# Attention scores on Trainium2: the second pass of two query tiles on the two row halves of TensorE

## The reference, cut to what matters

```python
q = _apply_rope((xn @ Wq + bq).reshape(b, s, 16, 64), cos, sin)   # k alike, v without rope
scores = einsum('bnqd,bnkd->bnqk', q, k) / sqrt(64)
scores = where(causal, scores, -1e9)
attended = einsum('bnqk,bnkd->bnqd', softmax(scores), v)
x = x + attended @ Wo + bo + int8_ffn(xn)
```

## Time and profile before

| | |
|---|---|
| timed, median of 3 | 1139.77 us (1139.35 to 1143.02) |
| profiled execution | 1136.91 us |
| its span, first to last instruction | 1134.8 us |
| TensorE busy | 1029.4 us (91%) |
| VectorE busy | 875.1 us (77%) |
| GpSimd busy | 752.3 us (66%) |
| ScalarE busy | 697.0 us (61%) |
| scores' first pass, L1592 | 512 matmuls, 148.2 us busy |
| scores' second pass, L1593 | 512 matmuls, 154.1 us busy |
| mask, L1594 | 512 matmuls, 112.6 us busy |

### The profile page before, as it was taken

The page is one execution under the profiler, slowest core; times in us unless marked ns, Lnnn a source line. Parts: engine busy times, 40 slices in busy tenths (PEclk is TensorE's granted clock), DMA queues, the critical chain, the costliest instruction groups (busy, mean ns, idle before and its releaser), DMA issues.

```text
span 1134.8 us, 23158 instructions
## 1 busy us (share of the span) xinstructions
PE 1029.4 (91%) x7950; PEld 667.2 (59%) x7950; DVE 875.1 (77%) x1846; ACT 697.0 (61%) x1864; POOL 752.3 (66%) x936
## 2 busy tenths in 40 slices
PE   3559887989999999999999999999999775999998
PEld 1236555656667666676667666676667542444444
DVE  7877768867887777777777777777776638999996
ACT  2248885656666666666666666666667415667763
POOL 2456656758777877778677877778676335666762
PEclk9789998999999999999999999999999977999999
DMA  8533333433332233233333233322331000000001
GB/s 274 162 88 94 107 125 109 137 95 95 112 103 85 90 117 111 86 103 94 94 102 104 89 94 107 113 85 93 96 100 51 1 1 1 19 20 19 19 28 48
DMA packets 100276, 98.47 MB, mean 87 GB/s; under 512 B 13888, under 2 KB 96064, under 8 KB 99520
## 3 DMA queue, kind: packets, MB, share of 16 engines
q1 hardware_dynamic: 100160, 96.99, 27.3%
HBM read 56.05 MB, written 40.90 MB: 85 GB/s over the span
## 4 chain that ended last, share of the span: by engine, by line
PE 73%; DVE 17%; ACT 4%; issue 3%; DMA 1%; POOL 0%; SPq 0%; DVEq 0%; ACTq 0%; POOLq 0%
PE bank L1521 24%; PE bank L1605 13%; PE bank L1619 12%; PE bank L1636 8%; PE bank L1592 6%; PE bank L1593 6%; DVE arena L1407 3%; PE bank L1594 2%; PE bank L1786 2%; DVE nm L1377 1%; ACT arena L796 1%; DVE wmax L1060 1%; DVE arena L1426 1%; DVE nm L1231 1%; DVE arena L1391 1%
## 5 line engine op out<-in xcount | busy, mean ns | idle before, releaser
L610 POOL TENSOR_SCALAR arena<-arena,rc 128x128 f32<-128x128 f32 (+3 forms) x512 | 279.2, 563 | 206.4 <-DVE rc L1239 206.4
L796 ACT ACTIVATE arena<-bank,nm 128x256 f32<-128x256 f32 (+3 forms) x512 | 268.9, 528 | 93.5 <-DVE nm L1231 83.7
L1231 DVE TENSOR_REDUCE nm<-bank 128x1 f32<-128x256 f32 (+3 forms) x512 | 229.9, 481 | 94.2 <-PE bank L1594 90.8
L1605 PE MATMUL bank<-ident,arena 128*128 128x128 f32 x1280 | 217.5, 278 | 19.7 <-ACT arena L804 17.9
L1605 PEld LDWEIGHTS bank<-ident,arena 128*128 128x128 f32 x1280 | 145.4, 142 | 56.1 <-ACT arena L804 23.6
L804 ACT ACTIVATE arena<-bank 128x256 f32<-128x256 f32 (+3 forms) x272 | 118.8, 440 | 79.4 <-PE bank L1605 79.2
L1592 PE MATMUL bank<-arena 128*128 128x256 f16 (+3 forms) x512 | 148.2, 302 | 10.7 <-ACT arena L796 10.0
L1593 PE MATMUL bank<-arena 128*128 128x256 f16 (+3 forms) x512 | 154.1, 301 | 0.0
L1619 PE MATMUL bank<-arena 128*64 128x512 f32 (+3 forms) x1024 | 152.0, 439 | 0.0
L1246 DVE COPY arena<-bank 128x512 f32<-128x512 f32 (+1 forms) x240 | 115.6, 482 | 29.0 <-PE bank L1605 25.5
L1619 PEld LDWEIGHTS bank<-arena 128*64 128x64 f32 x1024 | 67.8, 136 | 94.3 <-issue 72.2
(11 more groups left out here) (157 smaller groups left out, 2202.5 us busy)
## 6 DMA issues: line engine op xcount, KB each, us to landing
arena<-scr SPq DMA_DIRECT2D x320, 128.0 KB, 2.6
scr<-arena SPq DMA_DIRECT2D x256, 128.0 KB, 1.7
arena<-in_weights SPq DMA_DIRECT2D x5, 1024.0 KB, 7.1
x_sb<-in_x SPq DMA_DIRECT2D x8, 512.0 KB, 9.7
out<-x_sb SPq DMA_DIRECT2D x16, 256.0 KB, 2.1
xscr<-arena SPq DMA_DIRECT2D x12, 256.0 KB, 3.0
xsh<-xscr SPq DMA_DIRECT2D x6, 256.0 KB, 3.3
xsl<-xscr SPq DMA_DIRECT2D x6, 256.0 KB, 4.7
```

The costliest lines, as they stand in the source:

```text
L610: last = pool.tensor_scalar(pr[slot][:, OFF[i]:OFF[i + 1]], pr[slot][:, OFF[i]:OFF[i + 1]], rc[:, slot, i:i + 1], 1.0, ALU.mult, ALU.mult)
L796: act.activation(pr[slot][:, OFF[i]:OFF[i + 1]], s_tile[i], ACT.Exp, bias=nm[:, slot, i:i + 1], accum_out=sm[:, slot, i:i + 1]).then_inc(e ...
L1231: dve.tensor_reduce(nm[:, slot, i:i + 1], s_tile[i], AX.X, ALU.max, negate=True).then_inc(max_done, 1)
L1605: last = pe.transpose(banks[5 + h][:, (i - j) * P:(i - j + 1) * P], pr[2 * par + h][:, OFF[i] + j * P:OFF[i] + (j + 1) * P], ident[:])
```

## The change

The zero rows of `kz` go: kl now lies in both halves. The second pass of a tile uses 64 rows alone, rows 0 to 63 for odd tiles and 64 to 127 for even ones, so that two tiles' passes lie on different rows of the array and in different banks. For that the query stacks of even tiles are swapped (ql above, qh below); the projection of queries puts even tiles first (`by_parity`, `token_tiles`), so that `move_queries` can place the halves, in eight fetches of half size instead of four; `move_keys` makes eight fetches instead of six. The rotation tables get the same order, and two memsets go from GpSimd. On every engine scores are handled in two groups per head, (1, 0) and (3, 2), instead of three. (1, 0) waits for exps 0, 1 and 2 of the previous head. (3, 2) waits for exp 0 of its own head (`4 * g + 1`), which shares the bank sy. Core of the diff:

```diff
-        S_BANK = {1: 1, 0: 2, 2: 2, 3: 3}
+        S_GROUP = {0: 1, 1: 1, 2: 2, 3: 2}
+        Q_AT = {0: 0, 2: 1, 1: 2, 3: 3}
...
+        def by_parity(a):
+            return a.rearrange("p (e t c) -> p e t c", e=2, t=2)
+        def token_tiles(a, odd):
+            return a if odd else a.rearrange("p (t e c) -> p e t c", t=2, e=2)
...
         move_queries:
-                    sp.dma_start(qs[par][piece * HL:(piece + 1) * HL],
-                                 scr[par, 0, piece].rearrange("(h r) s -> r h s", h=4)).then_inc(q_in[par], 16)
+                    rows = scr[par, 0, piece].rearrange("(h r) s -> r h s", h=4)
+                    for e in range(2):
+                        at = (piece * HL + L * (1 - e)) % P
+                        sp.dma_start(qs[par][at:at + HL, :, e * 2 * P:(e + 1) * 2 * P],
+                                     rows[:, :, e * 2 * P:(e + 1) * 2 * P]).then_inc(q_in[par], 16)
...
         move_keys:
-                    if piece < 2:
-                        sp.dma_start(kd[par][at:at + HL], rows).then_inc(k_in[par], 16)
-                        sp.dma_start(kd[par][L + at:L + at + HL], rows).then_inc(k_in[par], 16)
-                    else:
-                        sp.dma_start(kz[par][at:at + HL], rows).then_inc(k_in[par], 16)
+                    both = (kd, kd, kz, kz)[piece][par]
+                    sp.dma_start(both[at:at + HL], rows).then_inc(k_in[par], 16)
+                    sp.dma_start(both[L + at:L + at + HL], rows).then_inc(k_in[par], 16)
...
         GpSimd:
-            for par in range(2):
-                pool.memset(kz[par], 0.0).then_inc(kz_zero, 1)
...
         ScalarE, ring:
-                exps(n + 1, 0, e, (1,))
+                exps(n + 1, 0, e, (0, 1))
                 v_whole(n)
                 pt_whole(n, 0)
                 high_e(n + AHEAD - 1)
-                exps(n + 1, 0, e, (0, 2))
...
                 high_o(n + AHEAD - 1)
                 pt_whole(n, 1)
-                exps(n + 1, 0, e, (3,))
+                exps(n + 1, 0, e, (2, 3))
...
-                exps(n + 1, 1, e, (1, 0, 2))
+                exps(n + 1, 1, e, (0, 1))
                 pt_whole(n, 3)
-                exps(n + 1, 1, e, (3,))
+                exps(n + 1, 1, e, (2, 3))
...
         VectorE, ring:
-                maxima(n + 1, 0, e, (1,))
+                maxima(n + 1, 0, e, (0, 1))
                 out_low(n - 1)
-                maxima(n + 1, 0, e, (0, 2))
...
-                maxima(n + 1, 0, e, (3,))
+                maxima(n + 1, 0, e, (2, 3))
...
                 pt_whole(n, 1)
                 even_terms(n + AHEAD)
                 inverse(n + 1, 0, e)
-                maxima(n + 1, 1, e, (1,))
+                maxima(n + 1, 1, e, (0, 1))
...
                     pt_whole(n, 2)
-                maxima(n + 1, 1, e, (0, 2, 3))
+                maxima(n + 1, 1, e, (2, 3))
...
         TensorE, scores:
-                after(pe, exp_done, 4 * g - 4 + {1: 1, 0: 3, 3: 4}[tiles[0]])
+                after(pe, exp_done, 4 * g - 1 if tiles == (1, 0) else 4 * g + 1)
                 for i in tiles:
-                    out, q = s_tile[i], qs[par][:, hh, i * P:(i + 1) * P]
-                    pe.matmul(out, q, kd[par][:, hh, 0:(i + 1) * P], start=True, stop=False)
-                    pe.matmul(out, q, kz[par][:, hh, 0:(i + 1) * P], start=False, stop=False)
-                    last = pe.matmul(out[:, i * P:(i + 1) * P], identb[:], maskb[:], start=False, stop=True)
+                    q = qs[par][:, hh, Q_AT[i] * P:(Q_AT[i] + 1) * P]
+                    pe.matmul(s_tile[i], q, kd[par][:, hh, 0:(i + 1) * P], start=True, stop=False)
+                for i in tiles:
+                    half = slice(L * (1 - i % 2), L * (1 - i % 2) + L)
+                    pe.matmul(s_tile[i], qs[par][half, hh, Q_AT[i] * P:(Q_AT[i] + 1) * P], kz[par][half, hh, 0:(i + 1) * P],
+                              start=False, stop=False)
+                for i in tiles:
+                    last = pe.matmul(s_tile[i][:, i * P:(i + 1) * P], identb[:], maskb[:], start=False, stop=True)
                 last.then_inc(s_done, 1)
```

## The result

The changed kernel takes 1200.17 us, median of 4 runs (1198.37 to 1201.71), against 1139.71 for the kernel before on the same chip: a ratio of the means of 1.0523 (95% interval 1.0498 to 1.0548), slower. The forecast was 1195 us. The profiled execution took 1199.76 us, of which 1197.8 are its span, 63.0 more than before.

A forecast was written before the change was run, and what follows sets the result against it. TensorE was taken to bound the rings. Per ring -0.43 - 0.19 + 0.84 + 0.63 = +0.85, +43 over 51 rings; with +7, +2 and some 3 at the ends, +55: 1195 us, range 1180 to 1218.

The forecast's parts named there:

- What the pass saves: Scores on TensorE: side-by-side second passes save 512 columns, 0.21 us per head, 0.43 per ring.
- The rival that they run one after the other: Second passes in scores: halves in different banks don't run side by side; 1217 us, chance 0.10.
- Two changes of form per group: Scores on TensorE: 0.10 us per change, 0.21 per group with weight loading, 0.84 per ring.
- the changes are free: Scores on TensorE: changes to half of the rows cost nothing, the wait stays; 1151 us, chance 0.15.
- run under other matmuls: Scores on TensorE: half-row passes change form free and run under the full matmuls around them; 1117 us, chance 0.07.
- The wait: Head 1's (3, 2): TensorE stands 0.63 us per ring for exp 0 of its own head.
- E: The end of a ring's `evens` on TensorE, from which the forecast counts times in us.
- The wait given back at `pt` 1: Six transposes before `evens`: they no longer wait for VectorE's copy of `pt` 0 of head 1, 0.19 us less.
- Steady rings: Rings 8 to 58, with `evens`, scores and `attended`: +0.85 us per ring, +43 over 51 rings.
- Rings 59 to 62: Last rings with scores, without `evens`: (1, 0) of head 1 stands too, 4 x 1.8 = +7 us.
- Rings 0 to 7: First rings, where ScalarE copies for both heads: part of the wait given back, +0.3 us each, +2.
- Ring -1: Before ring 0: `evens` now stands behind exp 0, some 3 us later.

The follow-up runs named there:

- x2: Changed kernel with both second passes of a group on the same half, rows 0 to 63, so they can't run side by side: 1221.69 us, ratio 1.0734.
- x3: Kernel before, order and waits untouched, with each tile's second pass on rows 0 to 63 alone: 1226.09 us, ratio 1.0773.
- x4: Changed kernel with head 1's wait removed by order: exp 0 made earlier, (3, 2) ahead of `pt` 3; half rows stay: 1156.14 us, ratio 1.0161.
- x8: Kernel before with head 1's `pt` 1 transposes moved behind the first three of the six products of `evens`: 1118.69 us, ratio 0.9831.
- x6: Changed kernel with SyncE's store of x's columns ahead of the query fetches instead of behind them: 1193.21 us, ratio 1.0494.
- x5: Changed kernel with the second pass on all 128 rows and the order in which head 1's (3, 2) doesn't wait: 1136.64 us, ratio 1.0004.
- x7: Kernel before, with its own data, zero rows and DMAs, in the new order of two groups without head 1's wait: 1136.47 us, ratio 1.0003.
- x1: Changed kernel with its second pass on all 128 rows again; groups, waits and DMAs stay: 1178.32 us, ratio 1.0355.

## Why the prediction was right

The sign and the size came out of the sum, and its steps in the steady rings hold, one of them with some luck:

- **What the pass saves.** 0.43 per ring: x2 puts 0.16 per (3, 2) group back when the halves may not run side by side, and its ordinary rings grow by 0.44. The rival that they run one after the other falls.
- **Two changes of form per group.** 0.10 each on rows as on columns, though no stretch of the rings before had shown rows. It was right to price them by `av` and not by the setup's 0.17, which set the upper end of the range. The granted clock was 1.00 there too, so the clock is no reason against that row. But 0.17 is a distance of starts that holds the one-column matmul itself, and the two instructions of this matmul, of one form, already start 0.14 apart (46.71 and 46.85). Groups take 0.59 and 0.92, forecast were 0.60 and 0.92. By x3 and x4 the two rivals fall in which the changes are free, or run under other matmuls. The Trainium skill, "TensorEngine Tiling (Array Packing)", Key Properties, says that a change of mode drains TensorE; the gaps agree, on both axes.
- **The wait.** Forecast was (3, 2) at E + 2.43 and its end at E + 3.35; measured are 2.45 and 3.38. x4 shows that it binds: with exp 0 made earlier and (3, 2) ahead of `pt` 3, 0.65 per ring go. It was found by walking VectorE's queue from E on, and in an ordinary ring that is the chain that comes second. Exp 0 goes behind ScalarE's copy of `pt` 2, which the forecast had ahead of exp 0 in every fourth ring only. That copy hangs on TensorE, so x2's 0.05 was not hidden. The size is right to 0.02 because both chains end within 0.1 us of each other; that is luck.
- **The wait given back at `pt` 1.** Six transposes in 0.66, and x8 gets the same gain by itself.
- **Steady rings.** +0.85 forecast, +0.88 measured, and the same in every fourth ring, as said. Rings 9 to 58 took 45.1 more; 43 were forecast for these and ring 8.
- **Rings 59 to 62.** +7 forecast, +7.6 measured.

Three terms were mis-sized, all of them outside the steady rings:

- **Rings 0 to 7, +2.** Measured +7.3 for rings 1 to 8, of which ring 8, a steady one in the forecast, has 1.0. The failed step is the one on what was costed at nothing: "SyncE has over 5 us free there". That was read from a steady ring. In the early rings SyncE also stores x's columns, and these stand behind the fetches; x6 takes back 5.9 of the 7.3. Rings 1 to 3 themselves came out at +0.33, near the +0.3 estimated.
- **Ring -1, +3.** Measured +4.5 up to the first `av`, ring 0 with it. I had counted the later start of `evens` and not the pace behind it:

```profile
66.62 0.93 PE L1601 MATMUL bank<-arena 128*128 128x512 f16 x2 [12.51 <-ACT arena L805]
...
68.20 0.63 PE L1528 MATMUL bank<-xsh,wh 128*128 128x512 f16 x1
68.63 0.63 PE L1528 MATMUL bank<-xsl,wh 128*128 128x512 f16 x1
```

TensorE now stands 12.51 us for the first exps, in one piece, and the products behind it start 0.43 apart per 512 columns, which is the 1.2 GHz level. Before, these `evens` ran ahead of the wait, from 56.66 on and 0.22 apart. How much of the 4.5 is pace and how much order was not separated: x5 and x7, with full rows in the new order of two groups, start the first `av` 2.4 and 4.0 later than the kernel before.
- **Behind the rings, 0.** Measured -1.5. Not followed up; x1 to x4 show -1.7 to -2.1, x5 to x7 -0.3 to -0.6.

The measured values in place of the forecast ones, 45.1 + 7.6 + 7.3 + 4.5 - 1.5, make 63 instead of 55, the whole of the span's difference. The steady rings and the last four have 3 of these 8 us, the three terms above the rest. By the profiled execution of before the forecast was 1192, and the changed one took 1199.76.

## What to carry to other kernels

A matmul on half of the array pays for changing the form before it and after it, here 0.21 us per group against the 0.05 to 0.16 us of columns that a pair of tiles saved: put all half-array work of a stretch together, or leave the zero rows in. When tiles are regrouped, look who now shares a bank with whom, and walk the queues of the engines that free it: the wait at the group cost 0.65 us per ring beside 0.84 for the forms, and a list of waits hid it. Where two queues meet at the instruction that is waited for, walk both. An issue queue that has time to spare in the steady state can be full in the first rings; price added DMAs there, by what is queued behind them.

## What the runs showed that I had not expected

A change between the whole array and 64 of its rows costs the same 0.10 us in each direction as one between the whole and 64 of its columns, although the halves of the rows then start 3 ns apart and add into banks of their own. And the zero rows, which look like waste, were cheaper than leaving them out: to take them from the kernel before with no other edit costs 7.7%.
